# Three added waits on GpSimd ahead of the output scatters of experts 5, 6 and 7

## The chip, the cores and the metric

The kernel runs on one core of one Trainium2 chip. The metric is the time of one execution on the device, in microseconds (us); less is better. Five engines work side by side: TensorE (PE in the profile, with its weight loads as PEld), VectorE (DVE), ScalarE (ACT), GpSimd (POOL) and SyncE (SP, which here only issues DMAs). Each runs its own instructions in the order in which they are written, and they wait for each other through semaphores.

## What is computed

One transformer layer on an input of 8 x 512 tokens of width 128, all in float32: a layer norm modulated by a condition, causal attention with 16 heads of 64 and relative positions, a gated residual, a second modulated layer norm, and a mixture of 16 experts. Each token goes to one expert, and each expert takes at most 256 tokens. The part that matters here:

```python
cap = -(-n_tok // n_exp)                      # 4096 / 16 = 256
idx = jnp.argmax(score, axis=-1)
pos = jnp.sum((jnp.cumsum(onehot, axis=0) - 1) * onehot, axis=-1)
keep = pos < cap
buf = jnp.zeros((n_exp, cap, d), x.dtype).at[idx, safe_pos].add(jnp.where(keep[:, None], xf, 0.0))
h = jax.nn.relu(jnp.einsum('ecd,edh->ech', buf, W1) + b1[:, None, :])
y = jnp.einsum('ech,ehd->ecd', h, W2) + b2[:, None, :]
out = y[idx, safe_pos] * gate[:, None]
out = jnp.where(keep[:, None], out, 0.0)
...
x = x + gb * _L0_ffn_ref(h, ...)
```

## The kernel before

The first 775 us are the attention of eight batches of 512 tokens (64 steps, one for each pair of heads). In it each batch's rows are also scattered to a buffer in HBM, `xbuf`, with 256 rows for each expert (L493 on GpSimd, `xbuf<-row,sidx`), so that the experts find their tokens in a row. After that come the 16 experts, e = 0 to 15, unrolled, each with a turn of some 3.4 us:

- **SyncE** loads the rows of expert e + 5 into a ring of five slots (`x<-xbuf`, L292) and, for the first eight turns, the weights of expert e + 8 (`raw<-in_w` L284, `prob<-in_w` L288). It waits for semaphore `ym` or `y` before each.
- **TensorE** computes the hidden layer (L1263, 12 products of 128x256, four groups of three, each group counted in semaphore `hm`), turns the next expert's rows (L1254), and computes the output (L1288, `bank<-prob,srow`, 16 records, in two halves t of 128 tokens). L1288 waits for the relus one by one.
- **ScalarE** makes four relus out of the four hidden groups (L833, `srow<-bank,smallT`). Each waits for its `hm` and raises semaphore `hr` by 1, so that `hr` is 4(e + 1) once expert e's relus are done. Then it rounds the next rows and weights (L824, L804).
- **VectorE** does the low parts (L1802, L1768) and the output: it copies the token numbers to `yidx` (L1814), adds the bias, multiplies with the gate and adds the residual (L1817, L1819, L1820, into `row` or `xh`). The last of these raises semaphore `y` by 2. Four output buffers and four `yidx` rows go round, e modulo 4. Before it writes `yidx` of expert e, VectorE waits for semaphore `ysc` of that buffer, that is, until the scatter of expert e - 4 has landed. Up to expert 4 the output of expert e is written in turn e + 1 (constant `LAGGING`, which is 5); in turn 5 the outputs of experts 4 and 5 follow each other, and from then on expert e's is written in turn e, up to expert 13.
- **GpSimd** does nothing in this stage but scatter the finished rows to their places in the output: function `expert`, two indirect DMAs (L583) for each expert, one for each half t, each behind `y`. A drain stands behind expert 9 and behind expert 15.

Nothing on TensorE or ScalarE waits for a scatter. The only readers of a scatter's completion are VectorE's wait for `ysc` four experts later and GpSimd's own wait at the end.

The functions with their line numbers:

Of the kernel before, what the change touches and what calls it, by code (L numbers as in the profile page):

```python
# [46 lines left out]
NB = FF // P  # L47
# [12 lines left out]
LAGGING = 5  # L60
# [15 lines left out]
def program(nc, x_d, xt_d, wall_d, wv_d, cols_d, wo_d, bo_d, wg_d, bg_d, w1_d, w2_d, b2_d, wmod_d,  # L76
            consts_d, ktab_d, iota_d, out_d):
    ctx = ExitStack()
    with ctx:
# [3 lines left out]
        def sem(name):  # L83
            return ctx.enter_context(nc.semaphore(name))
# [113 lines left out]
        s = {n: sem("s_" + n) for n in names}  # L198
# [178 lines left out]
        def _(gp):  # L377
# [200 lines left out]

            def expert(e, r):
                gp.wait_ge(s["yi"], e + 1)  # L580
                for t in range(ST):
                    gp.wait_ge(s["y"], ST * e + t + 1)
                    gp.indirect_dma_start(out=out_d.rearrange("b s d -> (b s) d"),  # L583
                                          out_offset=bass.IndirectOffsetOnAxis(ap=yidx[:, r, t:t + 1], axis=0),
                                          in_=ye[r][:, t, :], in_offset=None,
                                          bounds_check=last_token, oob_is_err=False).then_inc(s[f"ysc{r}"], 16)

            for e in range(E):
                expert(e, e % 4)
                if e in (9, E - 1):  # L590
                    gp.drain()
# [1333 lines left out]
```

## Time and profile before

| | us |
|---|---|
| median of 3 timed runs | 859.91 |
| lowest and highest of them | 859.32, 860.89 |
| the profiled execution | 866.42 |
| its span, first to last instruction | 864.3 |
| PE busy in the span | 852.5 (99%) |
| POOL busy in the span | 547.8 (63%) |

The timed runs are other executions than the profiled one. Times in the rows below are microseconds from the start of the span of the one profiled execution, which took 6.51 us longer than the median of the timed ones. In a row, the first two numbers are the start and the duration, then come engine, line, operation, output<-inputs, form and count. In brackets stands how long the engine had been idle before, and what released it; "issue" means that the profile shows nothing that it waited for. The ends of PE's instructions are modelled. A POOL row of L583 is the time in which GpSimd makes and issues the scatter, not the transfer.

### The profile page before, as it was taken

What the parts mean: (1) busy time and instruction counts of PE and PEld (TensorE: products, weight loads), DVE (VectorE), ACT (ScalarE), POOL (GpSimd) and SP (SyncE); (2) the same over time, 40 slices, a digit from 0 to 9 for tenths busy, and PEclk for the clock granted to TensorE, in tenths of its full rate; (3) what the DMA queues carried; (4) which work ended last, traced back from release to release, by engine and by line L of the source; (5) the groups of instructions that cost most, each with busy time, mean ns of one, the idle gap of its engine ahead of it and who ended that gap; (6) DMA issues with size and microseconds to landing.
All of it is one profiled execution on the core that took longest, in us unless ns stands there. A gap on an engine that the chain in (4) does not pass through costs nothing.

```text
span 864.3 us, 17499 instructions
## 1 busy us (share of the span) xinstructions
PE 852.5 (99%) x5532; PEld 681.4 (79%) x5532; DVE 658.3 (76%) x2041; ACT 723.6 (84%) x2008; POOL 547.8 (63%) x813
## 2 busy tenths in 40 slices
PE   8999999999999999999999999999999999999997
PEld 5877787777877778777787777877778877777996
DVE  7788788777878687777878787877878777877554
ACT  5888888888888888888988889888988888884653
POOL 6865565766567755776566765766667656673455
PEclk9999999999999999999999999999999999999999
DMA  8001970000000100000000000000000000015861
GB/s 288 10 1 28 266 172 14 13 20 19 14 13 1 38 2 14 13 20 18 13 13 14 14 14 13 1 21 2 13 14 13 12 13 14 2 35 187 298 209 38
DMA packets 25611, 41.40 MB, mean 48 GB/s; under 512 B 3334, under 2 KB 17527, under 8 KB 25136
## 3 DMA queue, kind: packets, MB, share of 16 engines
q1 hardware_dynamic: 22016, 33.86, 12.9%
q0 software_dynamic: 3072, 5.94, 1.9%
q8 instruction: 45, 0.74, 0.4%
q10 hardware_dynamic: 432, 0.49, 0.2%
q14 instruction: 46, 0.38, 0.1%
HBM read 25.93 MB, written 16.82 MB: 49 GB/s over the span
## 4 chain that ended last, share of the span: by engine, by line
PE 95%; DVE 1%; POOL 1%; issue 1%; ACT 1%; DMA 0%; POOLq 0%; DVEq 0%
PE bank L981 23%; PE bank L1014 17%; PE bank L939 17%; PE bank L994 16%; PE bank L1021 5%; PE bank L961 5%; PE bank L978 3%; PE bank L1288 3%; PE bank L1263 2%; POOL out L583 0%; PE bank L1029 0%; PE bank L887 0%; DMA x<-in_x 0%; PE bank L1050 0%; ACT prob L694 0%
## 5 line engine op out<-in xcount | busy, mean ns | idle before, releaser
L507 POOL TENSOR_SCALAR prob<-prob,rsum 128x128 f32<-128x128 f32 x508 | 261.4, 532 | 217.4 <-DVE rsum L1434 212.1
L694 ACT ACTIVATE prob<-srow,nmax 128x512 f32<-128x512 f32 (+3 forms) x512 | 285.9, 560 | 56.0 <-DVE nmax L1422 54.5
L1422 DVE CUSTOM_DVE_ANT_0 srow<-bank,consts 128x512 f32<-128x512 f32 (+3 forms) x512 | 246.7, 488 | 52.3 <-issue 39.6
L994 PE MATMUL bank<-consts,prob 128*128 128x128 f32 x1280 | 201.8, 272 | 0.0
L994 PEld LDWEIGHTS bank<-consts,prob 128*128 128x128 f32 x1280 | 158.3, 141 | 23.2 <-ACT pt L703 1.0
L703 ACT ACTIVATE pt<-bank 128x384 f32<-128x384 f32 x318 | 157.0, 497 | 11.5 <-PE bank L994 11.4
L1439 DVE SCALAR_TENSOR_TENSOR qx<-bank,qbias,consts 128x512 f32<-128x512 f32 x128 | 96.0, 750 | 72.8 <-PE bank L939 69.9
L1014 PE MATMUL bank<-pt,v 128*64 128x512 f32 x1008 | 149.6, 439 | 0.2 <-ACT pt L703 0.2
L981 PE MATMUL bank<-khi,qhi 128*128 128x512 f32 (+2 forms) x384 | 140.5, 366 | 0.5 <-DVE nmax L1422 0.3
L500 POOL TENSOR_TENSOR qlo<-qx,qhi 128x384 fp32r<-128x384 f32 x127 | 128.2, 1010 | 10.8 <-ACT qhi L661 4.3
L981 PE MATMUL bank<-khi,qlo 128*128 128x512 f32 (+2 forms) x384 | 130.3, 339 | 0.0
L981 PE MATMUL bank<-klo,qhi 128*128 128x512 f32 (+2 forms) x384 | 129.0, 336 | 0.0
L1014 PEld LDWEIGHTS bank<-pt,v 128*64 128x64 f32 x1008 | 67.4, 136 | 75.6 <-issue 59.5
L1446 DVE SCALAR_TENSOR_TENSOR klo<-bank,khi 64x512 fp32r<-64x512 f32 x128 | 87.9, 687 | 30.4 <-ACT kx L656 28.4
L694 ACT ACTIVATION_READ_ACCUMULATOR prob<-srow,nmax 128x1 f32 x512 | 97.4, 190 | 0.0
L661 ACT ACTIVATE qhi<-qx 128x384 fp32r<-128x384 f32 x128 | 66.4, 519 | 23.5 <-DVE qx L1439 22.3
L939 PE MATMUL bank<-hhi,whi 128*128 128x512 f32 x177 | 85.8, 485 | 0.0
L981 PEld LDWEIGHTS bank<-khi,qhi 128*128 128x128 f32 x384 | 72.4, 189 | 13.7 <-issue 1.7
L981 PEld LDWEIGHTS bank<-klo,qhi 128*128 128x128 f32 x384 | 72.6, 189 | 10.5
L655 ACT ACTIVATE khi<-bank 64x512 fp32r<-64x512 f32 x128 | 75.1, 586 | 2.3 <-PE bank L904 0.8
L981 PEld LDWEIGHTS bank<-khi,qlo 128*128 128x128 f32 x384 | 72.2, 188 | 5.1
L939 PE MATMUL bank<-hlo,whi 128*128 128x512 f32 x177 | 69.9, 395 | 0.0
(264 smaller groups left out, 1428.5 us busy)
## 6 DMA issues: line engine op xcount, KB each, us to landing
xbuf<-fill SPq DMA_DIRECT2D x4, 1540.0 KB, 23.6
x<-xbuf SPq DMA_DIRECT2D x13, 385.0 KB
raw<-in_w SPq DMA_DIRECT2D x16, 256.0 KB
prob<-in_w SPq DMA_DIRECT2D x16, 256.0 KB
h2T<-in_xt SPq DMA_DIRECT2D x8, 256.0 KB, 3.0
out<-row SPq DMA_DIRECT2D x8, 256.0 KB, 2.4
x<-in_x SPq DMA_DIRECT2D x1, 1536.0 KB, 12.8
modb<-mod_rows SPq DMA_DIRECT2D x1, 1536.0 KB, 7.2
```

What stands on the lines that cost most here:

```text
L500: gp.tensor_tensor(qlo[:, h, :], qx[:, h, P:S], qhi[:, h, :], ALU.subtract).then_inc(s["ql"], 1)
L507: end = gp.tensor_scalar(part, part, rsum[:, par, 4 * h + q:4 * h + q + 1], 1.0, ALU.mult, ALU.mult)
L655: act.activation(khi[0:HD, h, :], source[h * HD:(h + 1) * HD, :], ACT.Copy, scale=C_QKV)
L694: act.activation(prob[:, par, h, QOFF[q]:QOFF[q] + P * (q + 1)], srow[:, k % 4, 0:P * (q + 1)], ACT.Exp, bias=nmax[:, par, k:k + 1], scale ...
L703: act.activation(pt[:, h, KOFF[g]:KOFF[g] + GW[g]], source[:, 0:GW[g]], ACT.Copy)\
L939: last = pe.matmul(out, w[:, a, cols], h, start=(i == 0), stop=(i == 2))
L981: last = pe.matmul(out, a[:, h, (q - 1) * P:q * P], b[:, h, 0:P * (q + 1)], start=(i == 0), stop=(i == 2))
L994: last = pe.transpose(out[:, n * P:(n + 1) * P], prob[:, par, h, QOFF[q] + k * P:QOFF[q] + (k + 1) * P], ident)
L1014: last = pe.matmul(otb[h * HD:(h + 1) * HD, k * P:S], v[:, g, k, at + h * HD:at + (h + 1) * HD], pt[:, h, KOFF[k]:KOFF[k] + S - k * P], st ...
L1422: dve.tensor_tensor_reduce(out=srow[:, k % 4, 0:w], in0=scb[k % 2][:, 0:w], in1=mask[:, S - w:S], scale=-1.0, scalar=BIG, op0=ALU.add, op1 ...
L1439: dve.scalar_tensor_tensor(qx[:, h, :], prb[h][:, :], qbias[:, h, a:a + 1], qtab, ALU.add, ALU.mult).then_inc(s["qe"], 1)
L1446: dve.scalar_tensor_tensor(klo[0:HD, h, :], source[h * HD:(h + 1) * HD, :], C_QKV, khi[0:HD, h, :], ALU.mult, ALU.subtract).then_inc(s["kl ...
```

## The change

Three waits are added on GpSimd. Before the first scatter of expert e, for e = 5, 6 and 7, it now also waits for `hr` to reach 4(e + 3), which is the last relu of expert e + 2. Expert 8 and the later ones have no such wait; their scatters stand behind those of expert 7 in GpSimd's order, as before.

```diff
             def expert(e, r):
                 gp.wait_ge(s["yi"], e + 1)
+                if LAGGING <= e < LAGGING + 3:
+                    gp.wait_ge(s["hr"], NB * (e + 3))
                 for t in range(ST):
                     gp.wait_ge(s["y"], ST * e + t + 1)
                     gp.indirect_dma_start(out=out_d.rearrange("b s d -> (b s) d"),
```

GpSimd in the stage of the experts, from the scatters of expert 4 (buffer `row`) to those of expert 8 (`row` again). Before:

```order
787 L583 DMA out<-row,yidx 4096x128 [waits s_y,s_yi]
788 L583 DMA out<-row,yidx 4096x128 [waits s_y]
789 L583 DMA out<-row,yidx 4096x128 [waits s_y,s_yi]
790 L583 DMA out<-row,yidx 4096x128 [waits s_y]
791 L583 DMA out<-xh,yidx 4096x128 [waits s_y,s_yi]
792 L583 DMA out<-xh,yidx 4096x128 [waits s_y]
793 L583 DMA out<-xh,yidx 4096x128 [waits s_y,s_yi]
794 L583 DMA out<-xh,yidx 4096x128 [waits s_y]
795 L583 DMA out<-row,yidx 4096x128 [waits s_y,s_yi]
```

and now:

```order
787 L585 DMA out<-row,yidx 4096x128 [waits s_y,s_yi]
788 L585 DMA out<-row,yidx 4096x128 [waits s_y]
789 L585 DMA out<-row,yidx 4096x128 [waits s_y,s_hr,s_yi]
790 L585 DMA out<-row,yidx 4096x128 [waits s_y]
791 L585 DMA out<-xh,yidx 4096x128 [waits s_y,s_hr,s_yi]
792 L585 DMA out<-xh,yidx 4096x128 [waits s_y]
793 L585 DMA out<-xh,yidx 4096x128 [waits s_y,s_hr,s_yi]
794 L585 DMA out<-xh,yidx 4096x128 [waits s_y]
795 L585 DMA out<-row,yidx 4096x128 [waits s_y,s_yi]
```

No instruction moves on any engine: the rows are the same ones in the same order, and the first scatter of each of the experts 5, 6 and 7 carries `s_hr` as a third semaphore.

## Rows read from the trace of the kernel before

**Rows 1.** The page, part 4: the chain that ended last, shares by engine.

```profile
PE 95%; DVE 1%; POOL 1%; issue 1%; ACT 1%; DMA 0%; POOLq 0%; DVEq 0%
```

**Rows 2.** The chain in order of time, turns of experts 6 to 8.

```profile
823.96 0.79 issue
...
825.24 0.91 issue
```

**Rows 3.** ScalarE's relus in the timeline: experts 6, 7, 8, 9.

```profile
818.84 1.57 ACT L833 ACTIVATE srow<-bank,smallT 128x256 f32<-128x256 f32 x4 [1.04 <-issue]
...
822.26 0.98 ACT L833 ACTIVATE srow<-bank,smallT 128x256 f32<-128x256 f32 x2 [1.06 <-issue]
824.22 0.47 ACT L833 ACTIVATE srow<-bank,smallT 128x256 f32<-128x256 f32 x1 [0.97 <-PE bank L1263]
825.62 0.47 ACT L833 ACTIVATE srow<-bank,smallT 128x256 f32<-128x256 f32 x1 [0.93 <-remote]
...
828.89 0.47 ACT L833 ACTIVATE srow<-bank,smallT 128x256 f32<-128x256 f32 x1 [2.00 <-PE bank L1263]
...
832.92 1.57 ACT L833 ACTIVATE srow<-bank,smallT 128x256 f32<-128x256 f32 x4 [1.10 <-PE bank L1263]
```

**Rows 4.** GpSimd's scatters: first of 4, first of 5, second of 6, first of 7.

```profile
819.91 0.98 POOL L583 DMA_INDIRECT out<-row,yidx  x1 [1.35 <-DVE yidx L1814]
...
822.47 0.97 POOL L583 DMA_INDIRECT out<-row,yidx  x1 [0.31 <-issue]
...
826.29 0.97 POOL L583 DMA_INDIRECT out<-xh,yidx  x1 [0.30 <-issue]
830.81 0.97 POOL L583 DMA_INDIRECT out<-xh,yidx  x1 [3.54 <-DVE xh L1820]
```

**Rows 5.** Windows: PE, PEld, DVE, ACT, POOL busy, PEclk, DMA share, GB/s.

```profile
822.40:827.30 4.90, 3.20 (x23) 2.82 (x22) 1.72 (x5) 2.55 (x6) 3.88 (x4) 0.93 0.99 338
827.30:830.30 3.00, 3.00 (x17) 3.00 (x16) 1.66 (x5) 1.08 (x3) 0.00 (x0) 0.54 0.56 164
...
845.90:851.20 5.30, 4.79 (x37) 4.22 (x37) 2.92 (x8) 2.68 (x6) 4.30 (x4) 1.00 0.07 19
```

**Rows 6.** ScalarE's relus: expert 12, second of expert 13, expert 14.

```profile
843.28 1.57 ACT L833 ACTIVATE srow<-bank,smallT 128x256 f32<-128x256 f32 x4 [1.04 <-PE bank L1263]
...
847.67 0.47 ACT L833 ACTIVATE srow<-bank,smallT 128x256 f32<-128x256 f32 x1 [0.27 <-PE bank L1263]
...
852.16 1.57 ACT L833 ACTIVATE srow<-bank,smallT 128x256 f32<-128x256 f32 x4 [1.76 <-PE bank L1263]
```

**Rows 7.** GpSimd's scatters: first of experts 8, 9, 10, 11, 13.

```profile
834.76 0.97 POOL L583 DMA_INDIRECT out<-row,yidx  x1 [1.37 <-DVE row L1820]
...
838.18 0.97 POOL L583 DMA_INDIRECT out<-row,yidx  x1 [1.18 <-issue]
...
843.40 0.97 POOL L583 DMA_INDIRECT out<-xh,yidx  x1 [2.97 <-DVE yidx L1814]
...
845.95 1.26 POOL L583 DMA_INDIRECT out<-xh,yidx  x1 [0.30 <-issue]
...
854.30 0.97 POOL L583 DMA_INDIRECT out<-row,yidx  x1 [3.13 <-DVE row L1820]
```

**Rows 8.** GpSimd's four last scatters to xbuf: the third.

```profile
796.74 1.08 POOL L493 DMA_INDIRECT xbuf<-row,sidx  x1 [0.30 <-issue]
```

**Rows 9.** ScalarE's relus of expert 0.

```profile
796.35 1.57 ACT L833 ACTIVATE srow<-bank,smallT 128x256 f32<-128x256 f32 x4 [1.48 <-issue]
```

**Rows 10.** VectorE: output of expert 8 ends, of 9 ends, yidx of 10.

```profile
833.56 0.43 DVE L1820 TENSOR_TENSOR row<-row,x 128x256 f32<-128x256 f32 x1
...
836.98 0.42 DVE L1820 TENSOR_TENSOR row<-row,x 128x256 f32<-128x256 f32 x1
...
839.35 0.16 DVE L1814 CAST yidx<-x 128x2 uint32<-128x2 f32 x1
```

**Rows 11.** The last scatter of all, on GpSimd.

```profile
860.90 0.97 POOL L583 DMA_INDIRECT out<-xh,yidx  x1 [0.42 <-issue]
```

## The prediction

> **What bounds the kernel now.** I read the page's chain first. PE holds 95% of it [rows 1]; GpSimd, on which the change puts its waits, holds 1%, so a wait on GpSimd can only matter through what it does to TensorE. Then I went through the chain in order of time in the stage of the experts, looking for pieces that are not PE's. Two stand out, 0.79 and 0.91 us of "issue" in the turn of expert 7 [rows 2]. The relus show the same place. Experts 6 and 7 begin theirs 822.26 - 818.84 = 3.42 us apart, which is a turn's usual length. Expert 8's begin 828.89 - 822.26 = 6.63 us later, 3.21 too many, and expert 9's 832.92 - 828.89 = 4.03 later, 0.61 too many [rows 3]. So 3.82 us are lost there. Within expert 7 the third and fourth relu come late (824.22 and 825.62, where a turn without trouble makes all four in 1.57 us), each behind an idle time of 0.9 us and more. Behind that the granted clock falls: 0.54 on average in the 3 us from 827.30, so mostly the level of 1.2 GHz, after a stretch of 4.90 us in which PE was busy for only 3.20 [rows 5]. The reader should see one loss in two parts, late relus and then a slow clock that the gaps brought on.
>
> GpSimd's rows show what coincides. Its first scatter of expert 4 starts at 819.91, and from there six follow each other, those of experts 4, 5 and 6, to 826.29 + 0.97 = 827.26, with 0.3 us between them [rows 4]. They join because VectorE writes the outputs of 4 and 5 in one turn. At the same time the DMA engines are at a share of 0.99 [rows 5]. This is the place that the change spreads out.
>
> **The change, part by part.** *The three waits themselves* cost GpSimd nothing but time in which it has no other work: behind them stand only later scatters. On the clock of the trace before, expert 7's last relu ends at 825.62 + 0.47 = 826.09, expert 8's about 831.0, and expert 9's at 832.92 + 1.57 = 834.49 [rows 3]. A released scatter starts some 0.8 us later (output of expert 8 ready at 833.56 + 0.43 = 833.99, scatter at 834.76) [rows 7, 10], and a scatter takes 1.27 us with its gap. So expert 5 goes at 826.9 and 828.2, expert 6 at 831.8 and 833.1, expert 7 at 835.3 and 836.6. Expert 8 has been ready since 833.99, and follows at 837.8 and 839.1; expert 9 is ready at 836.98 + 0.42 = 837.40 [rows 10] and follows at 840.4 and 841.7. That is the first thing the edit does besides what it says: it takes the run of six apart at experts 4 to 6 and makes another one, of experts 7, 8 and 9, from 835.3 to 842.6.
>
> *Behind expert 9 stands a drain.* GpSimd was idle for 2.97 us there [rows 7], so expert 10 goes at about 842.6 + 3.0 = 845.6 instead of 843.40, experts 11 and 12 follow joined, as they did before (845.95 with a gap of 0.30) [rows 7], and the last of the six ends at 845.6 + 6 x 1.27 = 853.2. Expert 13's scatter started at 854.30 after 3.13 us of idleness [rows 7]. The delay is used up there, and the end (last scatter at 860.90 [rows 11]) stays where it was: 0 us.
>
> *VectorE's waits for landed scatters* are the only ones that the delay can reach. The tightest is `yidx` of expert 10 at 839.35 [rows 10], which wants expert 6's second scatter, now issued at 833.1: 6.2 us. The last scatter of all was issued at 860.90 and the span ended at 864.3, so a landing took at most 3.4 us with quiet queues. By then the weights' loads that fill the queues are largely through. I take 0 us; the bound above is the late landing among the rivals.
>
> *The late relus* are the term that decides, and no row shows what causes them. Below, the bound is the whole loss, -3.82 us, if the run of six is the cause and nothing replaces it. Above, it is the loss at the second run of six, experts 10 to 12 from 843.40: relus of experts 12 and 14 start 852.16 - 843.28 = 8.88 us apart [rows 6], 8.88 - 2 x 3.42 = 2.04 over two usual turns, with the clock at 1.00 and a DMA share of only 0.07 [rows 5]. If a run of six costs that, the new one at experts 7 to 9 does too: +2.04. Speaking for the run as cause: both losses begin with about its third scatter (822.47 and 845.95), and the second has no DMA load to blame. Speaking against: the four last scatters to `xbuf` also stand in one run, and during their third, at 796.74, expert 0's relus went by in 1.57 us undisturbed [rows 8, 9]. And the losses may belong to the profiled execution alone. It took 866.42 us, 6.51 more than the median of 859.91; the two losses make 3.82 + 2.04 = 5.86 of these. I take 0 us, because what is worth removing in the trace is so close to what the timed runs do not have.
>
> Two pages of the Trainium skill pull in opposite directions here. "SBUF — State Buffer", section "SBUF: two separate sides", says that only VectorE and GpSimd share a port and that TensorE and ScalarE never wait for anyone; by it GpSimd at work on a scatter cannot hold up PE, and the sum is 0, against the coincidence of rows 3 and 4. "Runtime: NRT & Kernel Launch", section "The ~15µs preamble/postamble breakdown", says that a profile's total lies about 6.2 us above the execution's own time whatever the kernel; by it the gap of 6.51 us would be bookkeeping, the losses would be in the timed runs as well, and the gain of 3.82 would be open. No row here decides between them.
>
> **The sum.** 0 for the waits, 0 for the drain and the end, 0 for the landings, 0 for the late relus: profiled 866.4, median 859.9 us.
>
> **The rivals.** *The run was the cause and leaves nothing behind*: 859.91 - 3.82 = 856.1 us. For it, the coincidence in time; against it, that the next run is made by the same edit.
>
> *The run was the cause and moves*: -3.82 + 2.04 = -1.78, 858.1 us. This is also the rival in which the edit does not do what it says: the pairs still join, only three experts later, with fewer loads in the queues. It lies on the border of what can be told from no change.
>
> *Slower*: the loss at expert 7 comes from full DMA queues (share 0.99) and stays, while the new run of experts 7 to 9 adds its own 2.04: 861.9 us. It decides from the point at which a run of six is enough without full queues, and rows 6 speak for that. Against it, again, rows 8 and 9.
>
> *A late landing*: should expert 6's scatter need more than 6.2 us, VectorE stands at `yidx` and the low parts of the next rows behind it; each us more costs PE one. At 8 us, 861.7 us.
>
> **How the numbers follow.** No change: 0.56. The run gone without a follower: 0.15. The run moved: 0.14, of which I count 0.08 as faster and 0.06 as no change. Slower by the new run: 0.11, by a late landing: 0.04. A measurement of this kernel can tell about 0.2% (1.7 us) from no change, so faster is 0.23, the same 0.62, slower 0.15. The range takes in no change (858.2 to 861.6) and goes down to the first rival's 856.1; left out are the cases of slower, 0.15. The likeliest case's own range is 858.2 to 861.6.
>
> **What the profile after would show.** Right about the mechanics: scatters of expert 5 start about 0.8 us behind expert 7's last relu, experts 7 to 9 are six scatters with gaps of 0.3, expert 13 has idle time before it again, and no wait of VectorE names a scatter. If the run was the cause, expert 7's four relus take 1.57 us, the clock stays at 1.00, and relus of experts 8 or 9 to 11 may come apart in its place. If that is seen and the timed runs do not move, the losses were the profiled execution's own. The forecast is wrong if the timed median falls below 858.2: then what the profile shows at expert 7 is in the timed runs too. It is wrong on the other side if `yidx` of experts 9 to 12 has a wait ahead of it.

## The result, and the profile after

| | before | changed | ratio, 95% interval |
|---|---|---|---|
| median of ten timed runs, us | 859.91 | 861.90 | 1.0024 (1.0015 to 1.0032) |
| lowest and highest | 859.32, 860.89 | 861.50, 863.18 | |
| the traced execution | 866.42 | 861.77 | |
| its span | 864.3 | 859.7 | |

The change makes the kernel 2.0 us slower, and at the same time its trace is 4.6 us shorter than the first one. Both are true, and the contradiction is the lesson of this case: the execution whose trace the prediction rests on was not like the timed ones. The changed kernel's traced execution, 861.77 us, lies among its timed runs; the first trace of the kernel before, 866.42, lies 5.5 us above the highest of its ten. The kernel before was executed 91 more times beside the experiments below, and its highest there is 861.27 us. Three executions stand apart, two of the kernel before at 1410.59 and 1411.05 us with a granted clock of 0.56 and one of e9 at 2514.03 us; the ratios leave them out, and they move no median given below by more than 0.04 us.

ScalarE's relus of experts 6 to 9 and of 15, timeline of the changed kernel (start, duration, engine, line, operation, tiles, form, count, idle before and releaser):

```profile
818.52 1.57 ACT L835 ACTIVATE srow<-bank,smallT 128x256 f32<-128x256 f32 x4 [1.07 <-PE bank L1265]
...
821.95 1.57 ACT L835 ACTIVATE srow<-bank,smallT 128x256 f32<-128x256 f32 x4 [1.07 <-PE bank L1265]
...
825.37 1.57 ACT L835 ACTIVATE srow<-bank,smallT 128x256 f32<-128x256 f32 x4 [1.06 <-PE bank L1265]
...
828.80 1.57 ACT L835 ACTIVATE srow<-bank,smallT 128x256 f32<-128x256 f32 x4 [1.06 <-PE bank L1265]
...
849.36 1.57 ACT L835 ACTIVATE srow<-bank,smallT 128x256 f32<-128x256 f32 x4 [1.58 <-PE bank L1265]
```

Against [rows 3] and [rows 6]: from expert 2 on every turn takes 3.43 us, all four relus of expert 7 follow each other, and nothing is late. (Experts 1 and 2 begin theirs 4.6 us apart, in this trace and in all the others, the first one included.) GpSimd's scatters in the same trace, the first of experts 5 and 7, both of 8 and 9, the first of 10 and of 13, and the last of all:

```profile
824.29 0.97 POOL L585 DMA_INDIRECT out<-row,yidx  x1 [2.48 <-issue]
...
831.14 0.97 POOL L585 DMA_INDIRECT out<-xh,yidx  x1 [0.96 <-issue]
...
833.91 0.97 POOL L585 DMA_INDIRECT out<-row,yidx  x1 [0.30 <-issue]
835.18 0.98 POOL L585 DMA_INDIRECT out<-row,yidx  x1 [0.30 <-issue]
836.47 1.09 POOL L585 DMA_INDIRECT out<-row,yidx  x1 [0.30 <-issue]
837.86 0.97 POOL L585 DMA_INDIRECT out<-row,yidx  x1 [0.30 <-issue]
841.77 1.24 POOL L585 DMA_INDIRECT out<-xh,yidx  x1 [2.94 <-issue]
...
849.83 1.07 POOL L585 DMA_INDIRECT out<-row,yidx  x1 [0.30 <-issue]
...
856.31 0.97 POOL L585 DMA_INDIRECT out<-xh,yidx  x1 [0.30 <-issue]
```

and VectorE's last output:

```profile
852.73 0.29 DVE L1840 TENSOR_TENSOR xh<-xh,x 128x128 f32<-128x128 f32 x1
```

Here the reader should look at what is not there. From 841.77 to the end GpSimd has no idle time but the usual gap of 0.30: twelve scatters in one row, where [rows 7] had 3.13 us of idleness before expert 13. The last output is ready at 853.02 and its scatter starts only at 856.31. So in this execution GpSimd's row of scatters sets the end, and TensorE's last product, which ends at 852.36, is 4 us ahead of it.

**Theory A**, formed on this trace: the three waits delay expert 9's scatters; the drain behind them carries the delay on to expert 10; behind the drain GpSimd can't catch up before expert 13, and what is left of the delay is the loss. **Rival B**: the late relus of the first trace belong to the kernel before, and something else in the changed one costs the 2 us. Further rivals are named with each experiment.

### The profile page after: what moved, and what is told of

Read it like the earlier page. It is cut to its first block and busy times, and to the rows that moved or that the text cites. A ratio compares the mean times of both kernels' runs of the same rounds, so it can differ in the third digit from the quotient of the medians.

```text
span 859.7 us, 17499 instructions
## 1 busy us (share of the span) xinstructions
PE 848.5 (99%) x5532; PEld 679.0 (79%) x5532; DVE 658.0 (77%) x2041; ACT 722.9 (84%) x2008; POOL 550.1 (64%) x813
```

## The experiments

One number puts all traces on one scale: how far the last scatter, and the end of the span, lie behind the first relu of expert 15, which TensorE's pace alone sets: in ten of the eleven traces below it comes 52.7 to 52.8 us behind the first relu of expert 0, with the added waits and without. That relu of expert 15 stands up to 1.8 us later in one trace than in another (1.0 because the stage begins later, 0.9 in e10, whose trace alone loses something within the stage, at expert 5), and the scale takes this out.

| kernel | last scatter behind that relu | end of span behind it | timed median |
|---|---|---|---|
| before, traced again (e1) | 853.87 - 848.99 = 4.88 | 8.31 | 859.95 |
| the changed kernel | 856.31 - 849.36 = 6.95 | 10.34 | 861.90 |
| waits at 5, 6 (e2) | 6.95 | 10.38 | 861.99 |
| wait at 7 (e3) | 6.94 | 10.40 | 861.86 |
| waits at 5, 6, 7, no drain at 9 (e4) | 4.89 | 9.13 | 860.63 |
| no waits, no drain at 9 (e5) | 4.88 | 9.15 | 860.87 |
| wait at 5 (e6) | 6.95 | 10.34 | 861.81 |
| waits at 5, 6, 7, 8 (e7) | 7.37 | 10.75 | 862.33 |
| waits at 5, 6, 7, drain at 4 (e8) | 5.68 | 9.47 | 861.20 |
| no waits, drain at 8 (e9) | 4.89 | 8.35 | 859.80 |
| no waits, drain at 11 (e10) | 5.73 | 8.97 | 860.95 |

The timed median less the third column is between 851.4 and 851.8 for ten of the eleven, and 852.0 for the last. So for ten kernels what is read behind expert 15's relus in these traces is, within some 0.3 us, what the timed runs lose. The last one, e10, loses some 0.4 us more in its timed runs than this scale shows. The kernel before was timed beside each group at 859.69 (e1 to e4), 859.94 (e5 to e8) and 859.76 (e9, e10).

### e1: the kernel before, traced again

No edit.

> The kernel before, once more, for a second trace. Theory A (GpSimd's row of scatters behind the drain sets the end): a trace without late relus, span about 857.8 us, expert 9's second scatter at about 835.4, expert 10's first at about 839.2, the last one at 853.3 to 854.3, so 2 to 3 us ahead of the 856.31 of the changed kernel. Rival B (the late relus of the first trace belong to every execution of this kernel): span above 862 again.

Measured: 859.95 us, a span of 857.3. The windows of its trace (PE, PEld, DVE, ACT, POOL busy, PEclk, DMA share, GB/s):

```profile
822.40:827.30 4.90, 4.90 (x45) 4.90 (x44) 3.12 (x8) 3.83 (x11) 3.68 (x5) 1.00 1.02 345
827.30:830.30 3.00, 3.00 (x29) 3.00 (x28) 1.96 (x6) 1.93 (x7) 1.88 (x3) 1.00 0.96 361
```

and GpSimd's scatters: first of expert 4, second of 7, first of 8, second of 9, first of 10, first of 13, and the last:

```profile
819.18 0.97 POOL L583 DMA_INDIRECT out<-row,yidx  x1 [1.19 <-DVE yidx L1814]
...
828.48 0.97 POOL L583 DMA_INDIRECT out<-xh,yidx  x1 [0.30 <-issue]
830.27 0.97 POOL L583 DMA_INDIRECT out<-row,yidx  x1 [0.81 <-DVE row L1820]
...
834.96 0.97 POOL L583 DMA_INDIRECT out<-row,yidx  x1 [0.30 <-issue]
838.85 1.22 POOL L583 DMA_INDIRECT out<-xh,yidx  x1 [2.92 <-DVE yidx L1814]
...
847.39 0.97 POOL L583 DMA_INDIRECT out<-row,yidx  x1 [0.80 <-DVE row L1820]
...
853.87 0.97 POOL L583 DMA_INDIRECT out<-xh,yidx  x1 [0.30 <-issue]
```

Rival B falls. Eight scatters in one row, longer than the six of [rows 4], with the DMA engines at 1.02, and PE is busy for 4.90 of 4.90 us where [rows 5] had 3.20, with the clock at 1.00. A run of joined scatters is not enough to slow TensorE, with full queues or without: the thing that the edit takes apart costs nothing in this execution, nor in those of e5, e9 and e10, whose traces have the same eight in a row. The idle time before expert 13 is 0.80, of which 0.30 is the usual gap: GpSimd has 0.50 us in hand there, not 3.13. From expert 10's start the rest is arithmetic. It moved from 838.85 - 848.99 = -10.14 to 841.77 - 849.36 = -7.59 us on the scale of the table, 2.55 later; less 0.50 makes 2.05; the last scatter moved by 6.95 - 4.88 = 2.07, the timed median by 1.99. Behind expert 13 there is next to nothing left to absorb a delay: e1's only other idle time is the 0.41 ahead of expert 15's first scatter, 0.11 more than the usual gap.

### e2, e3 and e6: which of the waits

```diff
e2
+                if e in (5, 6):
+                    gp.wait_ge(s["hr"], NB * (e + 3))
e3
+                if e == 7:
+                    gp.wait_ge(s["hr"], NB * (e + 3))
e6
+                if e == 5:
+                    gp.wait_ge(s["hr"], NB * (e + 3))
```

> The added wait before experts 5 and 6 alone. Theory A: expert 6's scatters end at about 830.2 and expert 7's follow at once, 831.5 at the latest for its first, 4 us later than without; little of it is given back before expert 9, so about as slow as the changed kernel if expert 7 queues: between 859.9 and 861.5 us. Rival C (the wait before expert 7 alone makes the loss): 859.9.

> The added wait before expert 7 alone. Theory A: expert 7 goes at 831.1, behind the relus of expert 9, as in the changed kernel, and experts 8 and 9 queue behind it; 861.9 us. Rival D (several waits, or the spacing of experts 5 and 6, add up to the loss): below 861.

> The added wait before expert 5 alone: a smaller dose. Theory A: expert 5 goes at 824.0 instead of 821.7, experts 6 to 9 queue behind it, expert 9 ends some 0.9 us later than in the kernel before, expert 10 starts 0.9 us later, 0.5 of it is absorbed by the idle time before expert 13: +0.4, about 860.1 us. Rival F (any of the waits brings the full 2 us, by another way than the backlog): 861.9.

Measured: 861.99, 861.86 and 861.81 us. The wait at expert 7 alone makes the loss, as theory A said. But so does the one at expert 5, of which it had expected 0.4 us, and e2 came out 0.5 above its bound. Either part alone is enough and together they are no worse, so rivals C and D (only one wait does it; they add up) both fall, and theory A lacked a term. The number of e6 is the one that rival F named (any wait brings the full 2 us, by another way than the backlog). Its trace shows the backlog all the same, twelve scatters behind the drain with no idle time but the usual gap, and e4 below, where all three waits stand and the loss at the last scatter is gone, speaks against another way. The term that theory A lacked is in the drain. The scatters of e6, first of expert 5, second of 9, first of 10, last:

```profile
824.09 0.97 POOL L585 DMA_INDIRECT out<-row,yidx  x1 [2.48 <-issue]
...
836.26 1.09 POOL L585 DMA_INDIRECT out<-row,yidx  x1 [0.30 <-issue]
...
841.50 1.31 POOL L585 DMA_INDIRECT out<-xh,yidx  x1 [4.14 <-issue]
...
856.11 0.97 POOL L585 DMA_INDIRECT out<-xh,yidx  x1 [0.30 <-issue]
```

Expert 9's second scatter is issued 836.26 - 834.96 = 1.30 us later than in e1 (0.17 of it is a later stage), but the idle time behind it is 4.14 us instead of 2.92. The lists of DMA issues, the last number being the us from issue to landing, show why. For this one scatter they have in e1 (issued at 834.96), in e6 (836.26) and in the changed kernel (837.86):

```profile
out<-row,yidx POOLq DMA_INDIRECT x1, 2.2
```

```profile
out<-row,yidx POOLq DMA_INDIRECT x1, 3.6
```

```profile
out<-row,yidx POOLq DMA_INDIRECT x1, 2.3
```

It lands at 834.96 + 2.2 = 837.2 in e1, at 836.26 + 3.6 = 839.9 in e6 and at 837.86 + 2.3 = 840.2 in the changed kernel, and expert 10 follows 1.7, 1.6 and 1.6 us behind that. The drain waits for landings, not for the issue alone. So a delay of 2.9 us in the issue (changed kernel) and one of 1.3 (e6) come to nearly the same landing, and to the same end.

Why the landing came late in e6 no run tests, but the traces point at the last load of rows (`x<-xbuf`). SyncE issues it 12.6 us ahead of expert 15's first relu in all three traces. It lands at 836.54 + 3.1 = 839.6 in e6 and at 836.74 + 3.1 = 839.8 in the changed kernel, and the scatter lands 0.3 to 0.4 us behind it both times. In e1 the scatter has landed at 837.2, before the DMA engines take up that load. If the scatter has to queue behind the load, every delay from 1.3 to 2.9 us ends at the same place, and only a larger one moves it on.

### e7: a larger dose

```diff
+                if 5 <= e < 9:
+                    gp.wait_ge(s["hr"], NB * (e + 3))
```

> The same wait also before expert 8: a larger dose. Theory A: expert 8 goes at about 834.6 instead of 833.9, expert 9 ends 0.6 to 0.9 us later than in the changed kernel, and all of it reaches the end: 862.5 to 862.8 us. Rival G (GpSimd's order behind the drain has a fixed cost that the delay only switches on): 861.9 as before.

Measured: 862.33 us. First scatter of expert 10, and the last:

```profile
842.94 0.97 POOL L585 DMA_INDIRECT out<-xh,yidx  x1 [2.76 <-DVE yidx L1816]
...
857.32 0.97 POOL L585 DMA_INDIRECT out<-xh,yidx  x1 [0.30 <-issue]
```

Against expert 15's relu at 849.95, expert 10 starts 0.58 us later than in the changed kernel and the last scatter 0.42 later; the timed medians say 0.43. The intervals of the two ratios overlap (1.0018 to 1.0040, and 1.0015 to 1.0032), but the fastest of the seven timed runs, 862.18 us, lies above the slowest of e6, 862.09, which was timed beside it. The loss grows again once the delay is large enough, which is against rival G (a fixed cost), though 862.33 is below the 862.5 to 862.8 expected.

### e4 and e5: the drain behind expert 9 taken out

```diff
-                if e in (9, E - 1):
+                if e == E - 1:
```

> The changed kernel without the drain behind expert 9. Theory A: the 2.94 us of the drain are gone from GpSimd's row, it catches up with VectorE before expert 14, and the end is that of VectorE's last output: 859.9 us or less. Rival E (the delay reaches the end in another way than through GpSimd's backlog): stays at 861.9.

> The kernel before without the drain behind expert 9. In the kernel before, GpSimd has caught up by expert 13 (idle 0.80 us ahead of it, 0.30 being the usual gap), so theory A expects nothing before the last scatters to change: last scatter at about 853.9, and 859.7 us. In the changed kernel without that drain, though, the span ran on 3.3 us behind the last scatter instead of 2.4; if this belongs to the missing drain, it shows here too: 860.5 us.

e4 has this edit in the changed kernel, e5 in the kernel before. Measured: 860.63 and 860.87 us. The last scatters, first e4, then e5:

```profile
854.76 0.97 POOL L585 DMA_INDIRECT out<-xh,yidx  x1 [0.30 <-issue]
```

```profile
854.23 0.97 POOL L583 DMA_INDIRECT out<-xh,yidx  x1 [0.31 <-issue]
```

On the scale of the table both stand at 4.9 us, exactly where the kernel before has its last scatter. So without the drain the three waits cost nothing (e4 is 0.94 us above the kernel before timed beside it, e5 0.93), and the delay reaches the end only where the drain takes from GpSimd the time to make it good: rival E falls. Still e4 missed its 859.9 and e5 both of its numbers, 859.7 and 860.5: it is 0.93 us slower than the kernel before, although nothing ahead of the last scatter is late. What grew is the time behind it, from the issue of the last scatter to the end of the span: 857.3 - 853.87 = 3.43 us in e1, 858.5 - 854.23 = 4.27 in e5. The drain in the middle earns 0.9 us at the end, and this is why it is worth its 2.9 us in a place where GpSimd has time.

### e8, e9 and e10: the drain moved

```diff
e8, with the three waits
-                if e in (9, E - 1):
+                if e in (4, E - 1):
e9, without them
-                if e in (9, E - 1):
+                if e in (8, E - 1):
e10, without them
-                if e in (9, E - 1):
+                if e in (11, E - 1):
```

> The changed kernel with the drain moved from behind expert 9 to behind expert 4, where GpSimd waits for expert 7's relus in any case (2.48 us of idleness in the changed kernel, the drain takes about 2.9). Theory A: the three waits cost nothing any more, expert 10 starts at about 839.3, the last scatter at about 853.9; 859.7 us, or up to 860.5 if a drain must stand late to keep the final one short. Rival F: 861.9.

> No added wait; the drain stands behind expert 8 instead of 9. GpSimd's row then has one more expert in which to catch up. Theory A: expert 9 is delayed by some 2 us, expert 10 by 1 or less, experts 13 to 15 go when their outputs are ready, the last scatter stands 4.9 us behind the first relu of expert 15 as in the kernel before: 859.9 us, no gain since nothing there was bound by it. A rival (the place of the drain matters in itself): more than 0.5 us either way.

> No added wait; the drain stands behind expert 11 instead of 9. Theory A: what counts is a delay that GpSimd can't make good before expert 13, whatever makes it. Expert 12 goes at about 846, experts 13 to 15 queue behind it in one row, and the last scatter comes at about 855.0 instead of 853.9: 861.0 us. If the added waits on the relus did harm in a way of their own, this kernel is as fast as the one before, 859.9.

Measured: 861.20, 859.80 and 860.95 us. e9 (ratio 1.000, interval 0.9991 to 1.0009) and e10 (1.0013, 1.0004 to 1.0022) came out as theory A said. e10 is the cleanest witness: it has no wait on relus at all, only a drain too late to be made good, and shows the same row of scatters to the end. Its timed median is 1.2 us above the kernel before. The trace accounts for 8.97 - 8.31 = 0.66 of these by the place of the end; where the other half comes from it does not show. Its first scatter of expert 12, behind the drain, and the last:

```profile
847.55 0.97 POOL L583 DMA_INDIRECT out<-row,yidx  x1 [2.92 <-DVE yidx L1814]
...
856.56 0.97 POOL L583 DMA_INDIRECT out<-xh,yidx  x1 [0.30 <-issue]
```

e8 missed by 0.7 us. The drain behind expert 4 does not hide behind the wait:

```profile
827.17 0.97 POOL L585 DMA_INDIRECT out<-row,yidx  x1 [5.19 <-ACT srow L835]
```

It is 5.19 us to expert 5 where the changed kernel has 2.48 by the wait alone, since at that time the DMA engines are full with weights and expert 4's scatters land late (5.2 us after the issue for the second of them in the changed kernel, where a scatter near the end of the stage takes 2.2). From 827.17 on GpSimd has no idle time any more, through 22 scatters, and is still 0.8 us behind at the last one.

## Why the prediction was wrong, point by point

**The mechanics of the waits were right.** The scatters of expert 5 were expected 0.8 us behind expert 7's last relu (824.29 against 821.95 + 1.57 = 823.52: 0.77), experts 7, 8 and 9 in a row of six (831.14 to 837.86), a drain of about 3 us (2.94), and no wait of VectorE for a landing. All of it is there. What it named beside them and what is not there is the idle time before expert 13: 0.30 us, the usual gap, at 849.83.

**The step that failed** is the one on the drain: "Expert 13's scatter started at 854.30 after 3.13 us of idleness [rows 7]. The delay is used up there, and the end (last scatter at 860.90 [rows 11]) stays where it was: 0 us." The delay itself was forecast at 2.2 us (expert 10 at 845.6 instead of 843.40) and measured at 2.55. The slack was wrong. Of those 3.13 us e1 has 0.80. Another 2.04 were there because TensorE had lost that much around expert 13 in that one execution, so VectorE's output came late while GpSimd went on. (The 3.82 lost earlier give no cover: expert 10's scatter starts 0.12 us behind expert 12's first relu in the first trace and 0.14 in e1.) A loss that the prediction refused to count as a gain, since the timed runs seemed not to have it, it took for granted as cover. Without them the slack is 0.50 us, and the term is 2.55 - 0.50 = 2.05 instead of 0. It could have been worked out from the rows at hand. At a turn of 3.43 us and 1.27 us for a scatter, GpSimd gains 3.43 - 2 x 1.27 = 0.89 us on VectorE with each expert; a drain of 2.9 us behind expert 9 therefore needs about three experts to be made good, and that leaves almost nothing before expert 13.

**The late relus** were put at 0 us, and that was right, for the reason given first: the timed runs don't have them. That a run of six scatters might be their cause is not borne out: e1 has eight in a row and no late relu. The rivals built on it (856.1 and 858.1) fall with it. The slower rival named 861.9 us, which is the measured time, but by a mechanism that isn't there; the number is a coincidence. The late landing didn't come either. No rival let GpSimd's backlog reach the end. The range then left out all the slower cases and ended at 861.6, 0.3 short.

**The two pages of the Trainium skill.** In e1 TensorE loses nothing beside eight scatters in a row, which agrees with "SBUF — State Buffer", section "SBUF: two separate sides", by which TensorE's port waits for no other engine. The gap of about 6.2 us that "Runtime: NRT & Kernel Launch", section "The ~15µs preamble/postamble breakdown", gives between a profile's total and the execution's own time is not in these numbers: the traced executions of the changed kernel (861.77) and of e1 (859.19) lie among their timed ones, and the kernel before has a span of 864.3 us in its first trace and 857.3 in e1, so that the difference lies within the execution. The gap could not explain the 6.51 us.

**What stays open** is what made the relus late in the first trace. None of the eleven traces taken after it shows it, so no run here could test a cause. The one loss within the stage that they do show, 0.90 us ahead of expert 5 in e10, is another: TensorE waits there for a load of rows, the clock stays at 1.00, and GpSimd's row of joined scatters has not begun.

```profile
813.93 0.44 PE L1254 MATMUL bank<-consts,x 128*128 128x128 f32 x2 [0.69 <-DMA x<-xbuf]
```

## What to carry to other kernels

Hold a trace against the timed runs before you read slack from it: if it is longer than the highest of them, its losses are suspect, and so is every idle time on other engines that these losses made. A wait on an engine off the critical path is free only up to the slack that it has behind its last synchronising point, here a drain: work out how much it gains in each turn and how many turns are left. And a drain belongs where nothing is in flight late and enough turns follow to make it good.

## What the runs showed that was not expected

- GpSimd's drain lasts until the last scatter has landed and 1.5 to 1.7 us more: 2.9 us idle with a landing 2.2 to 2.3 us after the issue (e1, the changed kernel; 2.79 in e9), 4.14 with 3.6 (e6). With the DMA queues full it came to 5.19 (e8).
- The time from the last scatter's issue to the end of the span grows with the number of scatters since the last drain: 3.24 us with 8 (e10), 3.38 to 3.46 with 12 (seven traces), 3.46 with 14 (e9), 3.79 with 22 (e8), 4.24 and 4.27 with all 32 (e4, e5). That is some 0.04 us for each. It is not the transfer that grows: the last scatter lands 2.2 us after its issue in the changed kernel (12) and in e5 (32) alike.
- The length of a scatter's row had no effect that shows on TensorE's pace in any trace behind the first: the turns beside it take 3.43 us, whether it has six, eight or ten.
